# Block attention: q and k projected once, operands fetched as 32-row blocks from DRAM

## The reference

```python
q = (h @ Wq.T + bq).reshape(B, S, 16, 8)      # k and v alike
scores = einsum('bihd,bjhd->bhij', q, k) / sqrt(8)
allowed = blk[:, None] >= blk[None, :]        # blk = arange(S) // 32
scores = where(allowed, scores, 0)            # forbidden scores are 0, not -inf
out = einsum('bhij,bjhd->bihd', softmax(scores), v).reshape(B, S, 128) @ Wo.T + bo
```

## Time and profile before

| | us |
|---|---|
| three runs: median (lowest to highest) | 1503.67 (1502.84 to 1507.27) |
| profiled execution: time | 1499.58 |
| profiled execution: span | 1497.8 |
| mean granted TensorE clock, share of full | 0.925 |
| TensorE busy | 1301.8 (87%) |
| ScalarE busy | 888.6 (59%) |
| VectorE busy | 819.5 (55%) |
| GpSimd busy | 291.6 (19%) |

### The profile page before, as it was taken

How to read it: one execution, slowest core, us unless ns; L and a number is a source line. 1 busy time by engine, 2 the same in 40 slices (tenths; PEclk the granted TensorE clock), 3 DMA queues, 4 the chain that set the end, 5 groups by cost and what they waited for, 6 DMA issues and landing times. The chain is left out here.

```text
span 1497.8 us, 25780 instructions
## 1 busy us (share of the span) xinstructions
PE 1301.8 (87%) x8997; PEld 920.7 (61%) x8998; DVE 819.5 (55%) x1414; ACT 888.6 (59%) x1584; POOL 291.6 (19%) x218
## 2 busy tenths in 40 slices
PE   3799999999999999999999996197196999999985
PEld 2577677777777777777777774065064545454443
DVE  6355445555555554564554563254477767676616
ACT  3577677777777777776777772032153456555563
POOL 3123113212311311321331130400431000000000
PEclk9799999999999999999999997599586789999997
DMA  5544245235334433533533442411103111111001
GB/s 158 134 112 115 64 101 121 60 90 121 86 77 109 114 77 92 120 74 76 120 91 73 118 114 92 135 44 44 54 1 71 44 44 44 44 44 44 16 1 34
DMA packets 58403, 118.71 MB, mean 79 GB/s; under 512 B 10674, under 2 KB 31668, under 8 KB 58164
## 3 DMA queue, kind: packets, MB, share of 16 engines
q1 hardware_dynamic: 56868, 113.37, 31.0%
q0 software_dynamic: 1424, 3.67, 0.8%
HBM read 18.64 MB, written 5.31 MB: 16 GB/s over the span
## 5 line engine op out<-in xcount | busy, mean ns | idle before, releaser
L524 DVE TENSOR_REDUCE a_negmax<-a_score 128x1 f32<-128x1024 f32 x257 | 314.2, 1223 | 402.4 <-PE a_score L357 402.4
L465 ACT ACTIVATE a_probs_T<-a_tr 128x512 f32<-128x512 f32 x514 | 279.7, 601 | 213.5 <-PE a_tr L363 210.0
L471 ACT ACTIVATE a_probs<-a_score,a_negmax 128x1024 f32<-128x1024 f32 x256 | 288.3, 1126 | 10.6 <-DVE a_negmax L524 10.5
L363 PE MATMUL a_tr<-ident,a_probs 128*128 128x128 f32 x2056 | 267.8, 273 | 0.4 <-ACT a_probs_T L465 0.4
L363 PEld LDWEIGHTS a_tr<-ident,a_probs 128*128 128x128 f32 x2056 | 238.0, 141 | 40.7 <-issue 10.2
L371 PE MATMUL a_out<-a_probs_T,a_v 128*64 128x256 f32 x2112 | 242.5, 382 | 0.5 <-issue 0.5
L1430 DVE TENSOR_REDUCE a_lowest<-a_score 128x1 f32<-128x512 f32 (+3 forms) x320 | 181.8, 631 | 83.1 <-PE a_score L1319 44.2
L1400 ACT ACTIVATE a_probs_T<-a_score_T 128x1024 f32<-128x1024 f32 (+1 forms) x192 | 146.4, 810 | 123.9 <-PE a_score_T L1295 87.9
L371 PEld LDWEIGHTS a_out<-a_probs_T,a_v 128*64 128x64 f32 x2112 | 146.1, 137 | 77.9 <-issue 10.7
L318 POOL TENSOR_TENSOR a_rden<-a_rden_col,a_ones 128x256 f32<-128x256 f32 x65 | 68.3, 1052 | 593.2 <-DVE a_rden_col L547 593.2
L1315 PE MATMUL a_score<-a_k_cur,a_q_still 61*128 61x512 f32 (+3 forms) x320 | 103.6, 435 | 8.5 <-DVE a_lowest L1430 6.8
(11 more groups left out here) (253 smaller groups left out, 1950.2 us busy)
## 6 DMA issues: line engine op xcount, KB each, us to landing
a_xn_cur<-normed_T SPq DMA_DIRECT2D x17, 512.0 KB, 5.0
a_q_rot<-a_q_raw SPq DMA_DIRECT2D x68, 128.0 KB, 2.4
a_k_rot<-a_k_raw SPq DMA_DIRECT2D x68, 128.0 KB, 2.3
a_k_stack0ah<-a_k_hi SPq DMA_DIRECT2D x18, 256.0 KB, 3.3
a_k_stack0al<-a_k_lo SPq DMA_DIRECT2D x18, 256.0 KB, 5.0
a_k_stack0bh<-a_k_hi SPq DMA_DIRECT2D x18, 256.0 KB, 5.0
a_k_stack0bl<-a_k_lo SPq DMA_DIRECT2D x18, 256.0 KB, 4.8
a_k_stack1ah<-a_k_hi SPq DMA_DIRECT2D x16, 256.0 KB, 3.3
```

What stands on the lines that cost most here:

```text
L363: last = nc.tensor.transpose(tr_ps[k // 4][:, k % 4 * P:k % 4 * P + P], probs[s % 4][:, k * P:k * P + P], core.ident[:])
L465: nc.scalar.activation(probs_T[(s - 1) // 4 % 2][:, h, 4 * i:4 * i + 4, tile % 2 * P:tile % 2 * P + P], tr_ps[i][:].rearrange("p (k q) -> ...
L471: nc.scalar.activation(probs[s % 4][:], score_ps[s % 2][:], ACT.Exp, bias=negmax[:, s:s + 1], accum_out=den[:, s:s + 1]).then_inc(probs_re ...
L524: nc.vector.tensor_reduce(negmax[:, s:s + 1], score_ps[s % 2][:], axis=AX.X, op=ALU.max, negate=True)\
```

## The change

- q and k are projected once, 8 pieces instead of 32, in batch order (`ORDER`); the high and low parts of all 128 columns stand in `q_hi`, `q_lo`, `k_hi`, `k_lo`.
- `store_rows` writes them to DRAM tensors of the form heads x 2 x 2 x 8 x 2048, each part twice, so that a head's 32 rows can be read back as one plain block; `load_rows` does that for every group.
- In the projection stage SyncE stores and loads only what group 0 needs (4 heads of batch 0). The other 12 heads of batch 0 and the loads of group 1 stand at the head of the attention stage's queue; batch 1 is stored in group 1's turn.
- Biases of q and k are loaded as columns. The output bias becomes a 1-row matmul that accumulates on each output projection.
- The weight transposes run under `normalize` (`pe_first`, `act_meanwhile`).
- The constants are loaded, and the constant rows of the operand tiles filled, in the expert stage: the DMA second in SyncE's queue, 14 fills on ScalarE after the routing exponential, `suffix` and its counts on GpSimd.
- The suffix sums stand at the end of the projection stage.

```diff
 def normalize(...):
             @block.tensor
             def _(pe):
+                if pe_first is not None:
+                    pe_first(pe)
...
                 nc.scalar.activation(root[:], var[:], ACT.Sqrt).then_inc(root_ready, 1)
+                if act_meanwhile is not None:
+                    act_meanwhile(act)
...
 def experts(...):
                 sp.dma_start(switch[:], sw).then_inc(small_loaded, 16)
+                operands.load(sp)
                 sp.dma_start(switch_b[:], ...).then_inc(small_loaded, 16)
...
+                operands.count(pool)
                 pool.wait_ge(places_ready, 1)
...
                 nc.scalar.activation(expd[:], shifted[:], ACT.Exp).then_inc(expd_ready, 1)
+                operands.fill(act)
...
+class BlockOperands:
+    def load(self, sp):
+        sp.dma_start(self.fixed[:], self.block).then_inc(self.fixed_loaded, 16)
+
+    def fill(self, act):
+        act.wait_ge(self.fixed_loaded, 16)
+        for tiles, i in ((self.q_still, 0), (self.q_moving, 0), (self.k_cur, 1)):
+            rows = self.fixed[:, 920 + P * i:920 + P * i + P]....broadcast_to([P, TB, P])
+            for pair in tiles:
+                for tile in pair:
+                    self.nc.scalar.activation(tile[:].rearrange("p (t k) -> p t k", t=TB), rows, ACT.Copy)
+
+    def count(self, pool):
+        self.nc.gpsimd.memset(self.suffix[:], 0.0).then_inc(self.suffix_cleared, 1)
+        pool.wait_ge(self.suffix_cleared, 1)
+        pool.wait_ge(self.fixed_loaded, 16)
...
 def block_attention(...):
+        def store_rows(sp, i, b, heads, stored):
+            rows, cols = slice(DH1 * heads.start, DH1 * heads.stop), slice(b * N, b * N + N)
+            for part in range(2):
+                for again in range(2):
+                    to = q_rows[heads, again, part, :, cols] if i == 0 else k_rows[heads, part, again, :, cols]
+                    sp.dma_start(to, parts[i][part][rows, cols].bitcast(F32)).then_inc(stored, 16)
+
+        def load_rows(sp, to, head_rows, m, landed):
+            for hp in range(2):
+                for x in range(2):
+                    rows = head_rows[m % G * HG + 2 * hp + x, :, :, :, m // G * N:m // G * N + N].rearrange("r p d n -> (r p d) n")
+                    sp.dma_start(to[hp][64 * x:64 * x + 32, :].bitcast(F32), rows).then_inc(landed, 16)
...
+            ORDER = [(i, 2 * b + c) for b in range(B) for i in range(2) for c in range(2)]
+                @block.sync
+                def _(sp):
+                    sp.wait_ge(stack_ready, 2)
+                    store_rows(sp, 0, 0, slice(0, HG), q_stored[0])
+                    sp.wait_ge(stack_ready, 4)
+                    store_rows(sp, 1, 0, slice(0, HG), k_stored[0])
+                    sp.wait_ge(q_stored[0], 64)
+                    load_still(sp, 0)
+                    sp.wait_ge(k_stored[0], 64)
+                    load_keys(sp, 0)
+                    load_moving(sp, 0)
...
-                load_still(0)
-                load_keys(0)
-                load_still(1)
-                load_keys(1)
-                load_moving(0)
+                store_rows(sp, 0, 0, slice(HG, H1), q_stored[1])
+                store_rows(sp, 1, 0, slice(HG, H1), k_stored[1])
+                sp.wait_ge(q_stored[1], 64)
+                load_still(sp, 1)
+                sp.wait_ge(k_stored[1], 64)
+                load_keys(sp, 1)
...
                     for t in range(4):
-                        ins = nc.tensor.matmul(score_ps[n % 3][:, t * D:t * D + D], attn_T[:, t * P:t * P + P], wo_T[:], start=True, stop=True)
+                        nc.tensor.matmul(score_ps[n % 3][:, t * D:t * D + D], attn_T[:, t * P:t * P + P], wo_T[:], start=True, stop=False)
+                        ins = nc.tensor.matmul(score_ps[n % 3][:, t * D:t * D + D], one_row[:], bo_row[:], start=False, stop=True)
```

More of the change, by code:

```diff
@@ L961, in load_all @@
[L961 to L966, removed]
+                sp.dma_start(bv_b[:], row(bv).broadcast_to([P, D])).then_inc(bias_loaded, 16)
@@ L977, in _ @@
                 @block.gpsimd
                 def _(pool):
-                    nc.gpsimd.memset(ones[:], 1.0)
+                    nc.gpsimd.memset(one_row[:], 1.0)
                     nc.gpsimd.memset(v_den[:, :, :, :, DH1:], 1.0)
[L981 to L987, removed]
-                            nc.gpsimd.tensor_copy(suffix[:, b, i, :, DH1].rearrange("p (g h) -> p g h", g=G), count)
@@ L999, in _ @@
-                    for i in range(4):
-                        ins = nc.tensor.transpose(w_ps[:, i * D:i * D + D], w[:, i, :], core.ident[:])
-                    ins.then_inc(wT_ready, 1)
-                    pe.wait_ge(rep_ready, 2)
-                    pe.wait_ge(zeroed, 1)
-                    for i in range(2 * G):
-                        ins = nc.tensor.matmul(b_ps[:, 2 * i:2 * i + 1], b_rep[:, i // G, i % G * HG:(i % G + 1) * HG].rearrange("o h r d -> o (h r d)"),
-                                               ones[0:1, 0:1], start=True, stop=True)
@@ L1007, in _, with project_v @@
-                    ins.then_inc(b_ready, 1)
-                    for k in range(STEPS):
-                        i, g, c = k // (4 * G), k // 4 % G, k % 4
+                    def project_v(q):
+                        if q >= 2:
+                            pe.wait_ge(v_added, q - 1)
+                        for t in range(4 * q, 4 * q + 4):
+                            ins = nc.tensor.matmul(v_ps[q % 2][:, t % 4 * D:t % 4 * D + D], core.xT[:, t * P:t * P + P], w_T[:, 2, :],
+                                                   start=True, stop=True)
+                        ins.then_inc(v_ready, 1)
@@ new lines, in _ @@
+                        if k >= 4:
+                            project_v(k - 4)
+                    pe.wait_ge(v_added, 4)
+                    pe.wait_ge(operands.fixed_loaded, 16)
+                    for bh in range(2 * B):
+                        b, half = bh // 2, bh % 2
+                        for kt in range(4 * half, TB):
+                            off = min(kt - 4 * half, 4)
+                            ins = nc.tensor.matmul(sums_ps[:, bh * P:bh * P + P], fixed[:, off * P:off * P + P], v_den[:, b, kt, :, 0:DH1],
+                                                   start=kt == 4 * half, stop=kt == TB - 1)
@@ L1064, in _ @@
[L1064 to L1069 removed]
+                    dve.wait_ge(bias_loaded, 64)
@@ L1070, in _ @@
+                    nc.vector.tensor_scalar(bq_scaled[:], b_col[:, 0:1], float(DH1) ** -0.5, None, ALU.mult).then_inc(bias_scaled, 1)
+                    for k, (i, c) in enumerate(ORDER):
+                        cols = slice(c * 512, c * 512 + 512)
                         dve.wait_ge(full_ready, k + 1)
                         if k % 2 == 1:
-                            nc.vector.tensor_scalar(high[k % DEPTH][:], full[k % DEPTH][:], part[:, 2 * i:2 * i + 1], None, ALU.mult).then_inc(high_ready[1], 1)
+                            nc.vector.tensor_copy(parts[i][0][:, cols], full[k % DEPTH][:]).then_inc(high_ready[1], 1)
@@ L1675 @@
         a[name] = nc.dram_tensor(f"in_{name}", arrays[f"in_{name}"].shape, F32, kind="ExternalInput").ap()
-    for name, value in (("rope", rope_tables()), ("part", part_signs()), ("block", block_consts())):
+    for name, value in (("rope", rope_tables()), ("block", block_consts())):
         arrays[f"const_{name}"] = value
```

217 lines of the change are left out of this document (87 added, 130 removed).

## The result

The changed kernel takes 1484.62 us (median of 4 runs, 1480.06 to 1485.93) against 1503.51 (4 runs, 1502.84 to 1507.27) of the kernel before on the same chip: a ratio of 0.9861, interval 0.9834 to 0.9889. It is faster by 19 us, where 30.5 were forecast; 1473 was predicted and 1463 to 1485 given as the range. The profiled execution of it was its fastest, 1480.06 us (span 1477.1). The measured time lies 0.4 us inside the upper end of the range and outside the forecast's own 1464 to 1479.

The account below looks back on a forecast made before the run. Bound: the projection stage by its number of 512-column pieces, attention by TensorE except VectorE in its lead. Terms -35.5 + 1.7 + 4.0 - 1.0 + 0.3 = -30.5 us, giving 1473 for the median; range 1463 to 1485.

Parts of the forecast that it names:

- Projection stage, -35.5: Before attention: 24 of 32 projection pieces and other work go, so the first score starts at 1106 instead of 1141.5 us.
- the bounds: First score's start: 1103.8 if compute ends last, 1110.4 if one tensor's DRAM stores run one after another; 1106 taken.
- the sign that the forecast had kept for rival 1: At the first score: waiting for a DMA from the row store, not the barrier after VectorE's suffix products, would show narrow stores.
- rival 1: Row stores to DRAM: 4 or 12 heads use only 4 or 12 engines, 13 GB/s each; total 1483 us, chance 0.20.
- Expert stage, +1.7: Expert stage: constants loaded ahead of the switch bias delay routing by 1.7 us (0.4 to 4.2); fills and GpSimd work hidden.
- Output bias, +4.0: Four output projections: four added 1-row matmuls each cost 1.0 us on TensorE, 4.0 in all; low end 2.
- rival 4: Projection stage: TensorE at half clock throughout, first score at 1118, -23.5 instead of -35.5; total 1485 us, chance 0.07.
- Clock at the head, -1.0: Attention's lead before the first transposed score: shorter idle gap may keep TensorE's clock up, -1.0 us (-5 to +2).
- the stores of the other heads, +0.3: Attention's start: twelve heads' stores queue before group 1's loads with 2.4 us spare; +0.3 us (0 to +5).
- the warm head: Attention's lead: TensorE's clock stays up throughout it, -5 us in place of -1; total 1469 us, chance 0.10.
- Rivals 2: Attention's lead: the clock stays up through it, -5 us in place of -1; total 1469 us, chance 0.10.
- 3: Attention: TensorE stays at half clock, each group costing 28 to 34 us more; two groups give 1533 us, chance 0.03.

Follow-up runs that it names:

- g2: Changed kernel with each output projection's four 1-row bias matmuls issued before its four products, instead of alternating with them: 1472.0 us, ratio 0.9793 to the kernel before.
- g3: The changed kernel run again unedited, on another chip, for a second profile: 1484.3 us, ratio 0.9866 to the kernel before.
- g4: Changed kernel with the output bias added to the residual on VectorE instead of by 1-row matmuls: 1468.8 us, ratio 0.9758 to the kernel before.
- e1: Changed kernel with the output bias and its 1-row matmuls left out altogether: 1472.4 us, ratio 0.9775 to the kernel before.
- f4: Changed kernel with switch bias loaded first, DRAM rows at one stride, moving rows issued later and output bias on VectorE: 1467.3 us, ratio 0.9746 to the kernel before.
- e2: Changed kernel with the output-bias matmuls given 128 rows (1/128 each) instead of 1 row: 1475.7 us, ratio 0.9789 to the kernel before.

## Why the prediction was right or wrong

- **Projection stage, -35.5: right in size, not in what ends it.** From the second normalization to the first score it was 72.4 us before and 35.5 after (33.8 in the second profile): -36.9 and -38.6. Put on the forecast's scale (3.1 us earlier), VectorE's last instruction ended at 1102.3, 1.2 before the 1103.5 that its steps gave, SyncE's last issue at 1104.0, and the first score started at 1104.6, between the bounds and 1.4 before the 1106 taken. But VectorE's products were not what it waited for last: it was released by the DMA of the k rows, the sign that the forecast had kept for rival 1, and in the second profile by the end of the stage behind SyncE's last issue (1105.63), 2.3 us after VectorE.
- **Expert stage, +1.7: too small by 2.** It was 3.3 in the first profile and 3.4 over all, 2.5 of them by the order of the two loads. With the stage before, -33.6 and -34.9 for the forecast's -33.8. The fills ended at 952.94 and hid, as forecast: 14 took 13.5 us, not 20. That the first score stood at 1107.68, where 1107.7 was named, is luck: this stage was some 1.5 us longer than forecast, and the next as much shorter.
- **Output bias, +4.0: this term failed.** The step "TensorE is the bound there: 4 x 1.0" used a duration that the earlier trace rows show for runs of equal instructions, and g2 finds it right for those: 2.25 us. But the changed kernel alternates the shapes, and no row of before showed an alternation of 128 rows with fewer. With the alternation and with the clock behind it, the term is 15.5 us (g3 against g4), 11.7 of it the projections themselves. Its low end, 2, and its high end, 4 x 1.16, were both reckoned from the same kind of row. Put 15.5 in place of 4.0 and the sum is -19.0, as measured. No rival had this cost. The range held the measured time only because its upper end was set by rivals 1 and 4, which are about other things: that is luck, not foresight. The Trainium skill, "TensorEngine Tiling (Array Packing)", section "Key Properties", says that changing the tiling mode drains TensorE. That matmuls of 128 rows and of 64 or fewer differ in this mode is an inference. With it the runs agree: 0.19 us per change, for 64 rows as for 1, and no such cost between 64 and 61.
- **Clock at the head, -1.0, and the stores of the other heads, +0.3: about right.** From 2 us behind the first score (1109.7) the clock was at 0.50 up to the first transposed score, so the warm head did not come; the first transposed score came 26.8 us after the first score (27.1 before), and no load of group 1 was late.
- **Rival 1, narrow stores: its mechanism is there, its price isn't.** The shares of 0.23 and 0.74 are those of 4 and 12 of 16 engines, as this rival had them, and the last k store, issued by 1096.8, had landed only at 1103.5. But an engine moved 89/(0.23 x 16) = 24 GB/s, not the 13 that the rows of before gave for copies inside SBUF, so the k rows were stored at 1100.4 on the forecast's scale and not at 1108.5. It cost 1.9 to 2.4 us of waiting. That the measured time lies near this rival's 1483 is a coincidence. Rivals 2, 3 and 4 did not come.

## What to carry to other kernels

Price an added matmul by its neighbours in the instruction stream, not by a run of its like: between matmuls of 128 rows and of 64 or 1 each change costs about 0.19 us here, so gather small ones, give them the neighbours' rows, or put them on an idle engine. The clock can fall behind such a stretch, so compare the granted clock of the stretches behind an edit too, and first of those ahead of it: only profiles that agree there can be compared behind it. When a kernel is compared by profile, take a second profile of each: two of the same kernel, on two chips, differed by 6.4 us in one stage here.

## What the runs showed of the hardware

- Four loads from DRAM into 32 rows are issued in 1.70 to 1.81 us where the queue is free, the same copies from SBUF in 2.43 and 2.54; they land in 2.5 to 2.6 us against 2.3.
- The last projection started at full clock in the kernel before, in e1, g4 and f4 and with 64 rows, and at or within a microsecond of half clock in the kernels with 1-row work, in whatever order. e2's, with 128 rows, was at half clock too (0.53 over it). Why stays open, and with it how the 4.7 us of the last one split into rows and clock.
- In g2, four accumulations were begun side by side in one bank of PSUM, and the size of its error (0.076 against 0.088) fits only one of them having kept its first term. The Trainium skill, "PSUM — Partial Sum Buffer", section "The four PSUM rules", says that a starting matmul clears the accumulate bits of the whole bank in the rows it writes; this agrees with three of four biases lost.
